# A two-block conditioned transformer on one core: the turned maxima copied by ScalarE instead of VectorE, and a batch's sums copied in one instruction

## The reference

```python
def _attention(x, padding_mask, qkv_w, qkv_b, proj_w, proj_b):     # x: (16, 128, 128)
    qkv = (x @ qkv_w.T + qkv_b).reshape(b, n, 3, H, HD).transpose(2, 0, 3, 1, 4)   # H = 16, HD = 8
    q, k, v = (qkv[0], qkv[1], qkv[2])
    attn = jnp.einsum('bhnd,bhmd->bhnm', q, k) * scale
    mask = padding_mask[:, None, :] & padding_mask[:, :, None]
    attn = jnp.where(mask[:, None, :, :], attn, -1000000000.0)
    attn = jax.nn.softmax(attn, axis=-1)
    out = jnp.einsum('bhnm,bhmd->bhnd', attn, v).transpose(0, 2, 1, 3).reshape(b, n, cdim)
    return out @ proj_w.T + proj_b
...
h = _modulate(_layernorm(x), shift_msa, scale_msa)
x = x + gate_msa[:, None, :] * _attention(h, padding_mask, qkv_w, qkv_b, proj_w, proj_b)
h = _modulate(_layernorm(x), shift_mlp, scale_mlp)
h = jax.nn.gelu(h @ fc1_w.T + fc1_b, approximate=True) @ fc2_w.T + fc2_b
x = x + gate_mlp[:, None, :] * h
```

## Time and profile before

| | |
|---|---|
| median of 3 runs | 177.81 us (177.63 to 178.04) |
| profiled execution, device time | 177.6 us |
| its span in the trace | 175.8 us |
| PE, PEld busy | 169.6 us, 132.5 us |
| DVE, ACT, POOL busy | 113.4 us, 109.2 us, 106.9 us |
| granted TensorE clock | full, in all 40 slices |

### The profile page before, as it was taken

The page is one execution under the profiler, slowest core; times in us unless marked ns, Lnnn a source line. Parts: engine busy times, 40 slices in busy tenths (PEclk is TensorE's granted clock), DMA queues, the critical chain, the costliest instruction groups (busy, mean ns, idle before and its releaser), DMA issues.

```text
span 175.8 us, 5695 instructions
## 1 busy us (share of the span) xinstructions
PE 169.6 (96%) x2244; PEld 132.5 (75%) x2244; DVE 113.4 (64%) x350; ACT 109.2 (62%) x282; POOL 106.9 (61%) x175
## 2 busy tenths in 40 slices
PE   6999999999999999999999999999999999999994
PEld 6986876794585988886688877888788765769594
DVE  0577899584014567798766876688888647695333
ACT  2588888907856262675676757668767796532600
POOL 5587989899935409719323434669989776690000
PEclk9999999999999999999999999999999999999999
DMA  4999999916963001100110010100000000001103
GB/s 106 370 413 438 412 414 421 395 39 130 188 229 142 4 2 65 62 6 6 65 63 5 6 45 20 65 6 6 4 7 6 6 2 4 0 0 60 63 0 119
DMA packets 5478, 19.31 MB, mean 110 GB/s; under 512 B 588, under 2 KB 1564, under 8 KB 4124
## 3 DMA queue, kind: packets, MB, share of 16 engines
q1 hardware_dynamic: 5132, 18.66, 29.2%
q10 hardware_dynamic: 320, 0.29, 0.6%
HBM read 7.24 MB, written 1.09 MB: 47 GB/s over the span
## 4 chain that ended last, share of the span: by engine, by line
PE 91%; DVE 3%; ACT 2%; issue 1%; DMA 1%; POOL 0%; POOLq 0%; DVEq 0%
PE ps L417 21%; PE ps L483 9%; PE ps L337 8%; PE ps L365 8%; PE ps L345 8%; PE ps L374 7%; PE ps L253 4%; PE ps L259 3%; PE ps L494 3%; PE ps L397 2%; PE ps L400 2%; PE ps L505 2%; PE ps L404 2%; PE ps L318 2%; PE ps L298 1%; DVE nm L1118 1%
## 5 line engine op out<-in xcount | busy, mean ns | idle before, releaser
L1118 DVE TENSOR_REDUCE nm<-ps 128x4 f32<-128x512 f32 x64 | 42.0, 683 | 16.8 <-PE ps L417 16.4
L835 ACT ACTIVATE shared<-ps 128x512 f32<-128x512 f32 x64 | 35.4, 601 | 16.3 <-PE ps L417 16.3
L417 PEld LDWEIGHTS ps<-k_pad,q_pad 32*128 32x128 f32 x512 | 29.7, 186 | 9.2 <-issue 5.8
L417 PE MATMUL ps<-k_pad,q_pad 32*128 32x128 f32 x512 | 35.0, 282 | 1.0 <-DVE nm L1118 0.5
L417 PE MATMUL ps<-q_pad,k_pad 32*128 32x128 f32 x512 | 35.1, 283 | 0.1
L417 PEld LDWEIGHTS ps<-q_pad,k_pad 32*128 32x128 f32 x512 | 29.4, 186 | 0.5 <-DMA q_pad<-nmT 0.3
L1244 POOL TENSOR_TENSOR rstd<-var_eps,half 128x4 f32<-128x4 f32 x16 | 16.4, 1023 | 19.7 <-DVE var_eps L965 16.5
L1329 POOL TENSOR_TENSOR gated<-attn,gate 128x128 f32<-128x128 f32 x16 | 7.4, 460 | 21.6 <-ACT attn L854 21.4
L483 PE MATMUL ps<-shared,vx 128*32 128x128 f32 x512 | 17.3, 275 | 0.1
L885 ACT ACTIVATE hid<-ps,W 128x512 f32<-128x512 f32 x16 | 10.9, 689 | 9.7 <-PE ps L365 9.7
L365 PE MATMUL ps<-hT,W 128*128 128x512 f32 x32 | 15.3, 599 | 0.0
(11 more groups left out here) (156 smaller groups left out, 335.5 us busy)
## 6 DMA issues: line engine op xcount, KB each, us to landing
q_pad<-gate SPq DMA_DIRECT2D x1, 4096.0 KB, 21.5
k_pad<-gate SPq DMA_DIRECT2D x1, 4096.0 KB, 30.7
gate<-gates SPq DMA_DIRECT2D x1, 2048.0 KB, 14.5
xs<-x SPq DMA_DIRECT2D x4, 256.0 KB, 5.8
gate<-mask SPq DMA_DIRECT2D x1, 1024.0 KB, 11.8
q_pad<-apT SPq DMA_DIRECT2D x4, 256.0 KB, 2.4
k_pad<-apT SPq DMA_DIRECT2D x4, 256.0 KB, 2.6
W<-weights SPq DMA_DIRECT2D x1, 768.0 KB, 9.9
```

The costliest lines, as they stand in the source:

```text
L417: return mm(bank(to)[:, t], held[some, t, b], moved[some, t, b], start=True, stop=True, skip_group_check=True)
L835: a(pT[b % 2][:, r], bank(of), ACT.Exp, scale=HD ** -0.5).then_inc(s["c_exp"], 1)
L1118: v.tensor_reduce(nm[b % 2][:, 4 * r:4 * r + 4], bank(of), AX.X, ALU.max, negate=True).then_inc(s["c_max"], 1)
```

## The change

It does two things to the second attention.

The copy of the turned maxima, bank 6 to `nmT`, goes from DVE to ACT in steps 2 to 15, that is for batches 1 to 14. ACT does it between exponential 2 and what followed that (`act_turned`). DVE's `turned_max` leaves the step; it stays ahead of the steps for batch 0 and behind them for batch 15. In its place DVE waits, from step 3 on and behind maximum 1, for ACT's copy (`c_nm`), so that DVE's next reading of bank 6 doesn't start before ACT's reading is over. SP's DMA waits for the same semaphore as before.

The sums of batches 0 to 12 are copied from bank 7 by one ACT instruction of 128x256 instead of two of 128x128.

```diff
             def back_o(b):
                 act.wait_ge(s["c_PV"], b + 1)
-                for e in range(2):
-                    a(oT[b % 2][:, e], ps[:, 7, N * e:N * e + N], ACT.Copy).then_inc(s["c_oT"], 1)
+                a(oT[b % 2][:].rearrange("c e n -> c (e n)"), ps[:, 7, 0:2 * N], ACT.Copy).then_inc(s["c_oT"], 2)
...
+            def act_turned(b):
+                act.wait_ge(s["c_NT"], b + 1)
+                a(nmT[b % 2][:], ps[0:16, 6, 3 * N:4 * N], ACT.Copy).then_inc(s["c_nm"], 1)
+
             def step(b):
                 if b >= 2:
                     weights_of(b - 2, 2, T_BANK[2])
+                    act_turned(b - 1)
                     if b < 6:
                         weights_of(b - 2, 3, T_BANK[3])
...
             def step(b):
                 maximum(b, 0, S_BANK[0])
-                turned_max(b - 1)
                 maximum(b, 1, S_BANK[1])
+                if b >= 3:
+                    dve.wait_ge(s["c_nm"], b)
                 if b == 3:
```

## The result

The changed kernel takes 178.61 us (median of 11 runs, 177.94 to 179.62), the kernel before in the same comparison 177.76 us (11 runs, 177.28 to 178.59). The ratio is 1.0044, with an interval of 1.0024 to 1.0065: slower by about 0.8 us, where 177.96 and no visible change were forecast. The profiled execution took 178.65 us, its span 176.9 (before 177.6 and 175.8).

A forecast was written before the change was run, and what follows sets the result against it. TensorE was taken as the bound, busy 169.6 us of 175.8. The terms 0 - 0 + 0.15 + 0 + 0 gave +0.15 us on the 177.81 us median, so 177.96 us; range 177.6 to 178.3.

The forecast's parts named there:

- In steps 6 to 15 ... cost 0: ACT idles for TensorE behind the first exponential; 0.33 us of cover hides the moved copy, cost 0.
- first slots don't wait for it except perhaps once: The DMA writing the maxima into the queries starts 0.07 us earlier; step 14's possible delay, 0 to 0.04 us, taken as 0.
- Step 3: ACT's copy moves vx by 0.16 us against 0.01 us of cover; batch 0's weighted sums load 0.15 us late.
- nothing takes this up again: TensorE is full after the late load of batch 0's weighted sums, so the 0.15 us stays.
- The copy hides in step 9: ACT's copy fills idle time behind the first exponential, 104.61 to 104.77, and the next copy's start at 104.94 stands; cost 0.
- The normalising: On DVE, behind maximum 1, it comes 0.20 us earlier without the copy; worth 0 on the path.
- The sums in one instruction: One ACT copy of 128x256, 381 ns, replaces two; 13 batches gain 0.05 us each on ACT, worth 0.
- no step is late at all: Rival: vx copies ready sooner, or the copy costs ACT little; the time stays 177.8 us; chance 0.28.
- The slower rival: ACT's copy doesn't overlap, 0.28 us instead of 0.16; steps 3, 5 and 14 cost 0.40 us: 178.2; chance 0.15.
- the conditions named for a failure: Steps 6 to 14 change length, second slots start at another distance behind the first maximum, or step 3 doesn't grow.

The follow-up runs named there:

- sums_only: The kernel before with only the sums of a batch copied by one ACT instruction instead of two; 178.03 us, ratio 1.0013 [0.9995, 1.0032].

## Why the prediction was wrong

**The step that failed is the sum over the steps outside 3: "In steps 6 to 15 ... cost 0", and the DMA's "first slots don't wait for it except perhaps once".** The sum counted the time of ACT's new instructions in the engine's queue, and left out that they are also 14 instructions more to be fetched while the kernel runs. At the last slot, which I hadn't looked at since the change doesn't touch it, TensorE already waited for a DMA in the trace of before, 0.34 us. There the term of 0 measured 0.60 us (the DMA) and 0.07 (the slot ahead), together 0.67, of the 0.85 us between the two medians. The rest isn't settled: the starts differ by 0.37 us in the two profiles, but that goes with the run, and the interval of the ratio (0.43 to 1.16 us) holds 0.67 by itself.

**Step 3 was also wrong, in the other direction.** That ACT's copy delays vx, and TensorE by 0.15 us, was the whole of the forecast sum. ACT's timeline in step 3, after (before in the earlier trace rows):

```profile
75.53 0.25 ACT L857 ACTIVATE nmT<-ps 16x128 f32<-16x128 f32 x1
75.69 0.57 ACT L835 ACTIVATE shared<-ps 128x512 f32<-128x512 f32 x1
76.17 0.44 ACT L807 ACTIVATE hc<-ps,shift,scale 128x128 f32<-128x128 f32 x1
76.51 0.41 ACT L820 ACTIVATE vx<-ps 128x128 f32<-128x128 f32 x2
```

And the weight load of the weighted sums (before in the earlier trace rows, put down to nobody):

```profile
76.97 0.27 PEld L483 LDWEIGHTS ps<-shared,vx 128*32 128x32 f32 x12 [0.21 <-ACT vx L820]
```

The price in the queue was right, 0.16 us (75.53 to 75.69), and so were the place and the 0.05 us from vx to the load (76.92 to 76.97). But the two vx copies took 0.41 us together instead of 0.46, so vx ended 1.14 us behind the second slot's start (75.78, below), where before it ended 1.04 behind (76.44 - 75.40): the load started 1.19 us behind it, for 1.11. Of 0.15 us, 0.08 arrived, and none of it stayed. The chain of after (the second slots and the maximum of before in the earlier trace rows):

```profile
75.78 1.17 PE ps L417 x32
76.97 1.08 PE ps L483 x32
...
79.20 0.70 DVE nm L1122
...
79.99 1.17 PE ps L417 x32
```

From second slot to second slot it is 4.21 us (75.78 to 79.99), before 4.22 (75.40 to 79.62). The 0.08 us went into idle time of the weight loads between the weighted sums and step 4's first slot, first before and then after:

```profile
77.59 0.18 PEld L417 LDWEIGHTS ps<-k_pad,q_pad 32*128 32x128 f32 x1 [0.27 <-issue]
```

```profile
77.98 0.18 PEld L417 LDWEIGHTS ps<-k_pad,q_pad 32*128 32x128 f32 x1 [0.20 <-issue]
```

That slot's first load comes 2.19 us behind the second slot's start before and 2.20 after, and the idle time ahead of it shrank from 0.27 to 0.20 us. What held this load before isn't shown (the profile names no releaser). So TensorE wasn't full there, and the sentence that "nothing takes this up again" was wrong.

**The rest held.** The copy hides in step 9, as the timeline of ACT after shows (before in the earlier trace rows):

```profile
104.49 0.60 ACT L835 ACTIVATE shared<-ps 128x512 f32<-128x512 f32 x1 [1.75 <-PE ps L417]
104.98 0.25 ACT L857 ACTIVATE nmT<-ps 16x128 f32<-16x128 f32 x1
105.30 0.28 ACT L843 ACTIVATE onT<-ps 128x128 f32<-128x128 f32 x1
```

onT starts 0.81 us behind the exponential, before 0.82; the copy takes 0.25 us, near to the 0.28 of the nearest rows. DVE in the same step:

```profile
104.45 1.29 DVE L1122 TENSOR_REDUCE nm<-ps 128x4 f32<-128x512 f32 x2
105.65 0.25 DVE L1132 RECIPROCAL rden<-ps 128x16 f32<-128x16 f32 x1
106.45 0.69 DVE L1122 TENSOR_REDUCE nm<-ps 128x4 f32<-128x512 f32 x1 [0.22 <-PE ps L417]
```

The normalising starts 1.20 us behind the first maximum, before 1.41: the 0.20 us are won, and spent in 0.22 us of waiting for TensorE, worth nothing, as forecast. The sums in one instruction take 384 ns (381 forecast), and no change from them shows (sums_only: 1.0013, with an interval that holds 1). The two small copies of ACT after, groups by form (before in the earlier trace rows):

```profile
L843 ACT ACTIVATE onT<-ps 128x128 f32<-128x128 f32 x16 | 4.4, 277 | 2.6 <-PE ps L505 2.2
L857 ACT ACTIVATE nmT<-ps 16x128 f32<-16x128 f32 x14 | 3.5, 251 | 0.1
```

Of the rivals, "no step is late at all" describes the steps themselves. The slower rival had the right sign and about half the size (0.40 us for 0.85), for a reason that wasn't there: the copy overlaps. Of the conditions named for a failure, one came, that step 3 doesn't grow. The other two, a change in steps 6 to 14 or at the second slots, didn't; the loss lies behind them, in a stage that no rival looked at.

## What to carry to other kernels

Before a change that alters how many instructions an engine issues, look in the trace for the instruction packets of that engine (about 130 instructions apart here), work out where they will fall after it, and see whether a small DMA for which TensorE waits with nothing else to do is in flight there. Take the instruction counts from the compiled kernel, not from the source (a semaphore raised by 2 cost an instruction more), and look where the packets fell in the new trace, since DVE's came 14 records later though its count hardly changed. And where a time changes that no step explains, a pad of instructions that do nothing is a cheap test; a DMA that is issued early enough is the better remedy than a lucky count.

## What the runs showed of the hardware

Blocks of some 8 KB of instructions are fetched while the kernel runs, and a DMA of 8 KB with one in its flight took 2.20 to 2.54 us in the chain where it was on it, for 1.66 to 1.67 undisturbed, in the profiles of seven runs and at three different DMAs (batches 12, 14 and 15). That the fetch is the cause is shown by moving it, with ACT's count and with DVE's, and by moving the DMA. A quarter of the DMA's packets waited until the fetch was over, which looks like one DMA engine that both use; the trace doesn't name the engines, and 0.23 of the 0.60 us after come behind the last packet and stay unexplained. Two increments at once cost an engine a semaphore instruction of its own, for the wait. A 16x128 copy out of the matmuls' memory took ACT 251 ns and a 128x128 one 277 in the same run, so fewer partitions saved little.
